# A four-layer graph network on one core: the eight spline weights of an edge move from PSUM to SBUF

## The reference

```python
h = jnp.maximum(_layernorm(x, axis=-1), 0.0)
# layer 0, per edge: k0 = 0, frac = edge_attr
w = jnp.where(bits_f[None] > 0, frac[:, None, :], 1.0 - frac[:, None, :])
weights = jnp.prod(w, axis=-1)                       # [E, 8]
xj = x[src]
z = (B[:, :, None] * xj[:, None, :]).reshape(Etot, S * x.shape[1])   # B holds the weights, S = 8
msg = z @ W.reshape(S * x.shape[1], W.shape[2])
agg = jax.ops.segment_sum(msg, dst, num_segments=x.shape[0])
out = agg / jnp.maximum(cnt, 1.0)[:, None] + x @ root
# then batch norm and elu; then layer 1 (attention), layer 2 (three graph convolutions), layer 3 (mean of neighbours)
```

## Time and profile before

| | us |
|---|---|
| median of 3 runs | 12690.88 |
| lowest, highest | 12641.61, 12698.97 |
| the profiled execution | 12644.07 |
| its span | 12642.2 |
| spline stage (159 to 3840) | 3681 |
| PE, POOL, DVE busy in the span | 8810.2, 7247.4, 4847.3 |
| mean granted clock of PE | 0.793 |

### The profile page before, as it was taken

How to read it: one execution, slowest core, us unless ns; L and a number is a source line. 1 busy time by engine, 2 the same in 40 slices (tenths; PEclk the granted TensorE clock), 3 DMA queues, 4 the chain that set the end, 5 groups by cost and what they waited for, 6 DMA issues and landing times.

```text
span 12642.2 us, 197864 instructions
## 1 busy us (share of the span) xinstructions
PE 8810.2 (70%) x46558; PEld 6095.1 (48%) x46559; DVE 4847.3 (38%) x11847; ACT 1810.1 (14%) x4731; POOL 7247.4 (57%) x6848
## 2 busy tenths in 40 slices
PE   4787777778784666666667764788378747864885
PEld 4787777777774444555555553222222222221222
DVE  5554444444446233333333334222322232234223
ACT  0000000000001233333333332000000000000000
POOL 3446665655554776666666662556455545664664
PEclk8888888888886677777777786888588868876887
DMA  7401111111111322222222221444244424433443
GB/s 286 155 17 14 14 13 13 13 13 13 12 12 25 62 61 60 59 60 58 57 56 56 56 54 38 146 148 150 57 149 151 137 77 146 154 115 105 149 153 90
DMA packets 577485, 1013.05 MB, mean 80 GB/s; under 512 B 342921, under 2 KB 352440, under 8 KB 577331
## 3 DMA queue, kind: packets, MB, share of 16 engines
q1 hardware_dynamic: 258819, 724.21, 17.0%
q0 software_dynamic: 316112, 286.92, 12.9%
q10 hardware_dynamic: 2400, 0.53, 0.0%
HBM read 862.36 MB, written 148.79 MB: 80 GB/s over the span
## 4 chain that ended last, share of the span: by engine, by line
PE 34%; another core or an unknown queue 31%; issue 15%; DVE 7%; DVEq 4%; DMA 3%; ACT 3%; SPq 1%; ACTq 1%; POOL 0%; POOLq 0%
PE psAB L800 13%; PE psCD L910 4%; PE psCD L909 4%; DMA R<-dense 2%; PE psCD L808 2%; PE psAB L853 2%; PE psCD L866 2%; PE psAB L859 1%; DVE one_hot L1118 1%; PE psCD L844 1%; ACT Q L702 1%; PE psAB L850 1%; PE psCD L781 1%; PE psAB L893 1%
## 5 line engine op out<-in xcount | busy, mean ns | idle before, releaser
L544 POOL DMA_INDIRECT gath<-sum_tab,idx_block x2688 | 2669.2, 993 | 2201.8 <-issue 1154.8
L800 PE MATMUL psAB<-one_hot,R 128*128 128x128 f32 x15680 | 2424.4, 316 | 633.6 <-DVE one_hot L1118 317.0
L800 PEld LDWEIGHTS psAB<-one_hot,R 128*128 128x128 f32 x15680 | 2254.6, 221 | 707.7 <-issue 658.2
L544 POOL DMA_INDIRECT gath<-spline_tab,idx_block x1568 | 1502.0, 958 | 1542.0 <-DVEq L1051 1058.1
L544 POOL DMA_INDIRECT gath<-gat_tab,idx_block x1568 | 1541.2, 983 | 1023.2 <-DVEq L1051 579.7
L909 PE MATMUL psCD<-R,Q 128*128 128x512 f16 x3528 | 1505.2, 427 | 563.3 <-DMA R<-dense 493.7
L518 POOL DMA_INDIRECT dense<-count_block,cell_block x900 | 1496.3, 1663 | 424.2 <-issue 268.8
L910 PE MATMUL psCD<-R,Q 128*64 128x512 f16 x3528 | 1555.3, 441 | 17.2 <-issue 17.1
L1343 DVE SCALAR_TENSOR_TENSOR R<-iota_row,tile_base,dstf 128x512 f32 x928 | 705.1, 760 | 1168.3 <-issue 1168.3
L893 PE MATMUL psAB<-gath,R 128*128 128x192 bf16 x3712 | 508.2, 276 | 822.7 <-DVE R L1343 406.6
L1324 DVE TENSOR_REDUCE row_part<-psAB 128x64 f32 x940 | 331.7, 353 | 1855.9 <-PE psAB L893 756.8
(11 more groups left out here) (252 smaller groups left out, 9263.1 us busy)
## 6 DMA issues: line engine op xcount, KB each, us to landing
R<-dense SPq DMA_DIRECT2D x504, 896.0 KB
dense<-stage SPq DMA_DIRECT2D x126, 896.0 KB
Q<-dst_rows SPq DMA_DIRECT2D x392, 256.0 KB
gath<-sum_tab,idx_block POOLq DMA_INDIRECT x2688
gath<-spline_tab,idx_block POOLq DMA_INDIRECT x1568
gath<-gat_tab,idx_block POOLq DMA_INDIRECT x1568
sum_tab<-Q SPq DMA_DIRECT2D x28, 672.0 KB, 5.5
dense<-count_block,cell_block POOLq DMA_INDIRECT x900
```

The source lines that it names most:

```text
L544: nc.gpsimd.indirect_dma_start(out=dest[:, s, j, :], out_offset=None, in_=table, in_offset=bass.IndirectOffsetOnAxis(ap=idx_block[:, c:c + ...
L800: nc.tensor.matmul(block, z[:, w, j, k * P:(k + 1) * P], oh32[:, j, :], start=(j == 0), stop=(j == J - 1))
```

## The change

`hat8` lies in `R`, behind `hat2`, in place of PSUM. The lists `cell_a` and `times_a` move up by 32 columns. Nothing else differs: the number and the order of all instructions are the same, on every engine.

```diff
@@ -162,7 +162,8 @@
         hat2 = R[:, o:o + 4 * J].rearrange("p (j a b) -> p j a b", a=2, b=2)
-        o += 4 * J
+        hat8 = R[:, o + 4 * J:o + 12 * J].rearrange("p (j a b) -> p j a b", a=2, b=4)
+        o += 12 * J
         cell_a, times_a = R[:, o:o + DP].bitcast(i32), R[:, o + DP:o + DP + DP // 2].bitcast(fp16)
@@ -216,7 +217,6 @@
         psE = pb("psE", 1024)
-        hat8 = psB[:, 0:KS * J].rearrange("p (j a b) -> p j a b", a=2, b=4)
         ps_turned, ps_product = (psA, psB), (psCD, psE)
```

## The result

The changed kernel takes 12,276.53 us (median of 4 runs, 12,263.96 to 12,298.34). The kernel before takes 12,694.67 us beside it (4 runs, 12,641.61 to 12,698.97). The ratio is 0.9682 with a 95% interval of 0.9652 to 0.9711: 418 us faster, where 121 us slower was forecast. The profiled execution of after took 12,272.46 us, with a span of 12,270.6 us.

The account below looks back on a forecast made before the run. No engine was full; PE's increments, held while POOL issues transfers back to back, were read as delaying the spline stage. Terms 0 + 0 + 5 + 116 = 121 us on 12,644, plus 47 to the median: 12,810 us, range 12,640 to 12,990.

Parts of the forecast that it names:

- The length of `z` and of `hat8`: DVE, spline stage: `z` stays at 2286 ns, `hat8` goes from 199 to about 192 ns; both counted as 0 us.
- The lock: Spline stage: a gather starting during the new `z` waits for it and ends 0.82 us after `z` does.
- The size of the lock: Spline stage: the second gather of each of 392 groups ends 0.85 us later, 333 us more of POOL.
- L518 stay at 1.62 us: Sign, spline stage: POOL's other transfer, L518, keeps its 1.62 us while the gathers' mean grows to about 1.16 us.
- The step that failed: Spline stage: PE's held increments come out 0.85 us later, 136 times, putting 116 us on the path.
- Faster: Rival, spline stage: the second gather's standstill lets held increments out early; about 12,590 us, chance 0.11.
- As a matter of supply, nothing: Spline stage: POOL's 333 us more fit in its 1058 us of waiting for slots, leaving 725; 0 us on the path.
- The later stages: Everything after the spline stage: as before, no change.

Follow-up runs that it names:

- f3: Against the kernel before: weights stay in PSUM, one 64-column GpSimd memset (0.92 us stop) after each spline group's first gather; chip E, 12,009.47 us, ratio 0.9688.
- e5: Against the kernel before: weights stay in PSUM, one 448-column GpSimd memset (1.24 us stop) after each spline group's first gather; chip C, 12,275.14 us, ratio 0.9693.
- e6: Against the kernel before: weights stay in PSUM, one 64-column GpSimd memset (0.92 us stop) after each spline group's first gather; chip C, 12,280.22 us, ratio 0.9699.
- f2: The changed kernel, unchanged, run again beside the kernel before on chip E; 12,078.49 us, ratio 0.9742.
- g1: The kernel before, unchanged, run again for a trace on chip F; 10,226.22 us, ratio 1.0002.
- g2: The changed kernel, unchanged, run beside the kernel before on chip F; 10,712.87 us, ratio 1.0482.

## Why the prediction was wrong

**The length of `z` and of `hat8`: right.** 2292 ns was measured for 2286, and 192 ns for 192. The Trainium skill ("VectorE: DVE Perf Modes", The TRN2 errata) gives 2291 ns for an fp32 tensor_tensor of 2048 numbers. The trace agrees with 2292.

**The lock: right as a mechanism.** A gather that starts 0.06 to 2 us into `z` ends 0.8 to 0.9 us after it: 0.86 in the rows above, 0.82 forecast. One that starts within about 0.04 us of `z` keeps its 0.95 us and makes `z` up to 0.07 us longer instead, as the forecast had it. The Trainium skill ("SBUF — State Buffer", Who interferes with whom) infers that tensor_tensor does not stall transfers that GpSimd issues. The trace does not agree: with both inputs of this tensor_tensor in SBUF, gathers took up to 3.08 us in place of 0.95.

**The size of the lock: wrong, 333 us forecast and 545 measured.** The forecast caught the second gather, 1.31 us into `z`, since POOL waited for DVE's slots and so started with `z`. Once POOL is nearly full, `z` starts when its rows have landed, and POOL's transfers meet it at another offset. Counted in the trace, 157 transfers started 0.50 to 0.75 us into `z` (16 before) and took 2.53 us on average; 190 had started within the first 0.25 us before, and now 56. It makes 1.39 us per group and not 0.85. Nor did L518 stay at 1.62 us, as forecast: 41 of its 360 transfers were caught too, and took up to 3.74 us (62 of the 545 us).

**The step that failed** is this: "If they come out when POOL's run ends, and the run is 0.85 us longer, then DVE's `one_hot` and PE start 0.85 us later". That increments are held was right. That a longer run delays them was wrong, because a transfer that is held up is itself a stop and lets them out. f3, e5 and e6 show it without the change: a stop of 0.92 or 1.24 us gives 0.969 to 0.970. The rival named *Faster* had this very mechanism, with 0.11 and a third of the cases. Against it stood only that a gap of 0.30 us lets nothing through, and that says nothing of a stop of 0.9 us and more. On chip E even such gaps let 8 to 30% out. Its size (103 us against 418) was low as well: it counted the freed increments at 4 us in a third of 136 cases, while the stage's mean group went from 9.39 to 8.38 us over all 392. Nor had the sum a term for the granted clock, which rose with PE's shorter waits and took 164 us off PE's busy time.

**"As a matter of supply, nothing": wrong.** It compared 333 us with 1058 us of waiting for slots. That wait was there because PE was late. When PE comes in time, POOL's 2622 + 585 us become the bound, and they cap the gain: 3207 of 3275 us. It is why the bare short stop can beat the change (f3's stage, 3203 us, is shorter than POOL's own 3233 us in f2), and on chip F, where POOL's work already fills the stage, the whole cost shows.

**The later stages: right.** They grow by 25 us in 8811.

What stays open is why chips D and F hold nothing. The program is the same, and so are its single operations: `z` takes 2286 ns in before on A and in g1 on F, and the median spline gather 947 ns on both. But over the whole span, "remote" waits add up to 8235 us on A (11 kinds, summed from the view) and to one of 5.2 us on F. Whether it is the chip or a state in which it was, no run tells. That it is PE's increments alone, and not those of DVE and ACT, is a count of the trace's updates (in the spline stage of before 99 in 100 of these came within 12 ns, and none later than 0.11 us). Why PE's increments are held is not shown.

## What to carry to other kernels

When a wait ends long after the instruction that should have ended it, look at what a third engine does in between and at when it stops. Then test it with a bare stop, before a layout is given the credit. A wait that is large because another engine is late is not slack: work out what each engine's own work makes of the stage once that lateness is gone. And repeat a gain on more than one chip: this change gives 3.2% and 2.6% on two chips and costs 4.8% on another.

## What the runs showed of the hardware

- On chips A, B, C and E, PE's semaphore increments came late while POOL issued indirect transfers 0.30 us apart (the longest such wait of `one_hot` is 8.4 us). On chip E stops of 0.8 to 1.1 us let 134 of 164 and 76 of 77 of them out, gaps of 0.30 us 8 to 30%. The held ones then came about 0.05 us after each other. On chips D and F none was late in the spline stage.
- The same kernel takes 12,694.67 us on A and 10,225.93 us on F, 24% more. In the spline stage it is 3672 against 2742 us; of these 930 us PE's busy time has 389, at a granted clock of 0.85 against 0.96, and the rest is waiting.
- TensorE's granted clock was lower in the stages in which PE waited more, held increments or not. On chip F it was 0.96 of full speed in g1's stage, where PE waited 250 us for `one_hot`, and 0.91 in g2's, where it waited 567 us.
- An indirect gather that meets a VectorE product with both inputs in SBUF ends 0.8 to 0.9 us after it, and took up to 3.08 us; beside the product with one input in PSUM it took at most 1.05 us.
- A GpSimd memset of 64 columns took 0.17 us, and the next indirect transfer began 0.75 us after its end.
